# One row of value products, and a second layer that is entered without phases

## The reference, cut to what matters

```python
h = shift_token(x)                        # second half of the channels, one token down
q, k, v = split(h @ wqkv)                 # 8 heads of 64
q = l2norm(q) * qs;  k = l2norm(k) * ks
q, k = rotary_xpos(q, k)                  # x*cos*scale + rotate_half(x)*sin*scale
attn = softmax(mask(q @ k.T))             # 128 queries, own and preceding window of 128 keys
x = x + (attn @ v) @ wo
h = layernorm(shift_token(x)) @ w1 + b1   # 682 + 682 wide
x = x + (a * gelu(g)) @ w2 + b2
```

## Time and profile before

| | |
|---|---|
| runs | 1597.18, 1601.13, 1603.43 us; median 1601.13 |
| profiled execution | 1595.59 us, of which span 1593.7 us |
| busy share of the span | PE 93%, DVE 75%, ACT 65%, POOL 46% |
| chain that ended last | PE 79%, DVE 9%, ACT 4%, issue 4%, POOL 3% |
| mean granted TensorE clock | 0.971 of full speed |
| stage 0, attention 1, FFN 1 | to 269, to 707, to 918 us |
| attention 2, FFN 2 | 929 to 1370, to the end |

### The profile page before, as it was taken

How to read it: one execution, slowest core, us unless ns; L and a number is a source line. 1 busy time by engine, 2 the same in 40 slices (tenths; PEclk the granted TensorE clock), 3 DMA queues, 4 the chain that set the end, 5 groups by cost and what they waited for, 6 DMA issues and landing times.

```text
span 1593.7 us, 35524 instructions
## 1 busy us (share of the span) xinstructions
PE 1478.7 (93%) x10355; PEld 1209.0 (76%) x10355; DVE 1196.0 (75%) x3393; ACT 1030.2 (65%) x2610; POOL 735.2 (46%) x897
## 2 busy tenths in 40 slices
PE   7899991899999999979999949999999999799996
PEld 6468871688888888858888838888888888588885
DVE  6762786788888888885656458888888888766664
ACT  5223574688888888865454428888888888445553
POOL 4003255566555656532222145566665665244442
PEclk9999996999999999989999979999999999999998
DMA  5002134000000000002000020000000000000101
GB/s 176 1 1 85 77 113 116 16 7 5 5 5 5 5 5 5 5 8 88 8 13 7 14 63 5 6 5 5 5 5 5 6 5 6 30 27 28 53 27 53
DMA packets 57522, 44.04 MB, mean 28 GB/s; under 512 B 13214, under 2 KB 55386, under 8 KB 57442
## 3 DMA queue, kind: packets, MB, share of 16 engines
q1 hardware_dynamic: 57442, 43.07, 8.8%
HBM read 26.24 MB, written 8.39 MB: 22 GB/s over the span
## 4 chain that ended last, share of the span: by engine, by line
PE 79%; DVE 9%; ACT 4%; issue 4%; POOL 3%; DVEq 1%; ACTq 0%; DMA 0%; POOLq 0%; SPq 0%; PEldq 0%
PE bank L1892 8%; PE bank L1860 7%; PE bank L1806 7%; PE bank L1819 7%; PE bank L1725 6%; PE bank L1727 6%; PE bank L1726 6%; PE bank L1753 4%; PE bank L1955 4%; PE bank L1957 3%; PE bank L1956 3%; PE bank L1970 2%; PE bank L1605 2%; PE bank L1972 2%; PE bank L1971 2%
## 5 line engine op out<-in xcount | busy, mean ns | idle before, releaser
L1199 ACT ACTIVATE prob<-prob,neg_max 128x256 f32<-128x256 f32 x512 | 254.8, 502 | 0.2
L784 POOL TENSOR_TENSOR rnorm<-sumsq,neg_half 128x8 f32<-128x8 f32 x128 | 212.9, 1664 | 23.5 <-POOL sumsq L781 23.5
L798 POOL TENSOR_TENSOR qk_cos<-qk_cos,qk_sin 128x512 f32<-128x512 f32 x128 | 180.5, 1411 | 45.9 <-DVE qk_cos L2354 45.9
L1725 PE MATMUL bank<-wqkv_hi,hT_hi 128*128 128x512 f32 x384 | 177.3, 462 | 5.6 <-DVE hT_lo L2340 5.6
L1955 PE MATMUL bank<-h_hi,w_hi 128*128 128x512 f32 (+1 forms) x352 | 143.1, 406 | 12.5 <-POOL h_lo L839 12.5
L1727 PE MATMUL bank<-wqkv_hi,hT_lo 128*128 128x512 f32 x384 | 154.3, 402 | 0.0
L1726 PE MATMUL bank<-wqkv_lo,hT_hi 128*128 128x512 f32 x384 | 154.0, 401 | 0.0
L1121 ACT ACTIVATE qk_sq<-bank 128x512 f32<-128x512 f32 x128 | 76.9, 601 | 116.0 <-PE bank L1727 116.0
L1333 ACT ACTIVATE act_hi<-act_full 128x512 fp32r<-128x512 f32 x96 | 60.8, 634 | 137.3 <-DVE act_full L2677 137.3
L1232 ACT ACTIVATE pT<-bank 128x512 f32<-128x512 f32 x256 | 138.8, 594 | 10.6 <-PE bank L1892 3.4
L1892 PE MATMUL bank<-pT,v_sb 128*64 128x128 f32 x2048 | 140.2, 279 | 0.5 <-ACT pT L1232 0.5
(11 more groups left out here) (276 smaller groups left out, 3940.0 us busy)
## 6 DMA issues: line engine op xcount, KB each, us to landing
x_sb<-in_L_attn_hidden_states SPq DMA_DIRECT2D x8, 512.0 KB, 7.0
x_in<-in_L_attn_hidden_states SPq DMA_DIRECT2D x8, 512.0 KB, 4.8
x_scratch<-x_in SPq DMA_DIRECT2D x8, 512.0 KB, 3.0
f_x<-x_scratch SPq DMA_DIRECT2D x8, 512.0 KB, 4.0
out<-f_y SPq DMA_DIRECT2D x8, 512.0 KB, 3.0
raw<-in_L_ffn_w SPq DMA_DIRECT2D x6, 640.0 KB
hs<-x_sb SPq DMA_DIRECT2D x16, 224.0 KB
hs<-x_sb SPq DMA_DIRECT2D x64, 56.0 KB
```

Of the source, the lines that this page charges most:

```text
L784: pool.tensor_tensor(rnorm[:, part * HEADS:(part + 1) * HEADS], sumsq[:, which * HEADS:(which + 1) * HEADS], neg_half[:, 0:HEADS], ALU.pow ...
L1199: act.activation(prob[:, h], prob[:, h], ACT.Exp, bias=neg_max[:, h:h + 1], scale=-1.0, accum_out=psums[:, h:h + 1]).then_inc(exped, 1)
L1725: pe.matmul(bank[:, to], hT_hi[:, c], wqkv_hi[:, c, cols], start=(c == 0), stop=False)
```

## The change

It has three parts.

1. A second tile `pT_far` takes the place of spare memory, so that all four pieces of `probs_out` have a home, and PE does V1 V0 V2 V3 without a break.
2. The order of the pieces in `step` is new on every engine. PE projects block `n` in step `n` (before: `n-1`), weighs, turns and multiplies block `n-2` (before: `n-3`). POOL weighs two heads (before one), DVE three (before four). The orders of heads (HIDDEN, EXPED and so on) change with it.
3. Both barriers between layer 1 and 2 are gone. The tiles of the FFN lie elsewhere (`hn`, `h_full`, `gelu_sb`, `act_full`), so the tables can be made during the FFN: POOL makes the scales and all eight table pieces behind its last work of layer 1, then stages block 0. PE turns block 0 between the last two `down` of the last group, ACT and DVE take it out, and PE projects it right behind the last `down`. DVE's last `add_up` stands behind `lo(0)`. ACT clears the tiles in step 0. The last move into `hs` is waited for by POOL only before its loop.

```diff
@@ tiles
+        pT_far = place("pT_far", [P, 2, 4 * P])
-        place("spare", [P, 10 * P])
+        place("spare", [P, 2 * P])
@@ PE, step
-                    if live(n, 4):
-                        project_out(n - 4)
-                    if live(n, 1):
-                        project(n - 1, 1, qk_raw[1])
-                    if live(n, 2):
-                        scores(n - 2, 0)
-                    if live(n, 3):
-                        turn_probs(n - 3, 0)
-                        turn_probs(n - 3, 1)
-                    if live(n, 1):
-                        project(n - 1, 0, qk_raw[0])
-                    if live(n, 3):
-                        turn_probs(n - 3, 2)
-                        turn_probs(n - 3, 3)
-                        values(n - 3, 0)
-                        values(n - 3, 1)
-                    if live(n, 2):
-                        scores(n - 2, 1)
-                    if live(n, 3):
-                        values(n - 3, 2)
-                        values(n - 3, 3)
...
+                    if live(n, 1):
+                        turn_qk(n - 1, 0)
+                    if live(n, 0):
+                        transposes(n)
+                    if live(n, 3):
+                        project_out(n - 3)
+                    if live(n, 0):
+                        project(n, 1, qk_raw[1])
...
+                        values(n - 2, 1)
+                        values(n - 2, 0)
+                        values(n - 2, 2)
+                        values(n - 2, 3)
+                    if live(n, 1):
+                        scores(n - 1, 1)
+                    if live(n, 0):
+                        turn_qk(n, 1)
+                        project(n, 2, v_raw)
@@ PE, entry of layer 2
+                if lay:
+                    down(lay * NG - 1, FC - 2)
+                    pe.wait_ge(act_ready, FC * (lay * NG - 1) + FC - 1)
+                    transposes(0, ahead=True)
+                    down(lay * NG - 1, FC - 1)
+                    pe.wait_ge(act_ready, FC * lay * NG)
+                    pe.wait_ge(ffn_split, SPLITS * lay)
@@ POOL, end of FFN 1
-                    end_phase(pool, 4 + 2 * lay)
+                    scales(lay + 1)
+                    for a in range(2):
+                        for i in range(2):
+                            for h in range(2):
+                                table(a, i, h).then_inc(sc_made, 1)
+                    pool.wait_ge(hs_moved, moved_in(lay + 1) - 48)
+                    pool.wait_ge(w2_used, FC * (lay * NG + NG - 1))
@@ DVE, entry of layer 2
+                if lay:
+                    lo(0, ahead=True)
+                    add_up(lay * NG - 1, NG - 1)
+                    dve.wait_ge(sc_made, MADE + 2 * TABLES + 8)
@@ ACT, step (the part round the exponents)
+                    if live(n, 2):
+                        exponent(n - 2, 6)
+                    if live(n, 1):
+                        k_out(n - 1, 1 - i)
+                    if live(n, 2):
+                        exponent(n - 2, 7)
+                    if live(n, 0):
+                        hi(n)
```

More of the change, by code:

```diff
@@ L58 @@
 SPLITS = 4 + NG // 2
+TABLES = 6
 def hs_slot(t):
@@ new lines, in table @@
+                def table(a, i, h):
+                    operand = (raw[:, 2, 0:BPB * 64], sin_raw[:].rearrange("p a n -> p (a n)"))[a]
+                    return pool.tensor_tensor(rope[:, :, a, i, 32 * h:32 * h + 32], operand.rearrange("p (t k d) -> p t k d", t=BPB, k=2)[:, :, i, :],
+                                              sc_x[:, a, i, 32 * h:32 * h + 32][:, None, :].broadcast_to([P, BPB, 32]), ALU.mult)
+                if not lay:
+                    scales(0)
+                    for i, h in ((0, 0), (0, 1), (1, 0)):
+                        table(1, i, h)
+                    end_phase(pool, 3)
@@ L1278, in step @@
                         weigh(n - 2, 7)
+                        probs_out(n - 2, 0)
                         weigh(n - 2, 5)
-                for n in range(6):
-                    step(n, n % 2)
-                with act.Fori(3, NB // 2) as u:
+                        probs_out(n - 2, 1)
+                    if live(n, 1):
+                        exponent(n - 1, 1)
+                    if live(n, 0):
+                        square(n, 0)
+                    if live(n, 2):
+                        probs_out(n - 2, 2)
+                        probs_out(n - 2, 3)
+                    if live(n, 1):
+                        exponent(n - 1, 3)
+                        exponent(n - 1, 0)
+                        v_out(n - 1, 1 - i)
+                    if live(n, 2):
+                        values_out(n - 2)
+                    if live(n, 1):
+                        exponent(n - 1, 2)
+                for n in range(4):
+                    step(n, n % 2)
+                    if lay and n == 0:
+                        act.activation(warm[:], warm[:], ACT.Exp).then_inc(gate_exp, 1)
+                        act.wait_ge(w2_used, FC * NG * lay)
+                        clear()
+                with act.Fori(2, NB // 2) as u:
                     for i in range(2):
                         step(u * 2 + i, i)
-                for n in range(NB, NB + 3):
+                for n in range(NB, NB + 2):
                     step(n, n % 2)
@@ L1353, in _ @@
                     group(NG // 2 - 1, i, False, last)
-                if not last:
-                    act.activation(warm[:], warm[:], ACT.Exp).then_inc(gate_exp, 1)
-                    end_phase(act, 4 + 2 * lay)
-                else:
+                if last:
                     last_norm(NG - 1, 1, NG // 2)
@@ L1653, in _, with down, transposes @@
             end_phase(pe, 2)
+            def down(k, j):
+                w = fw(j)
+                pe.wait_ge(act_lo_ready, FC * k + j + 1)
+                if j == 0:
+                    pe.wait_ge(x_ffn, 1 + 2 * k)
+                for i in range(GB):
+                    to = bank[:, 4 + i // 2, (i % 2) * D:(i % 2 + 1) * D]
+                    tok = slice(i * P, (i + 1) * P)
+                    pe.matmul(to, act_hi[0:w, j % 3, tok], w2_hi[0:w, j], start=(j == 0 and i % 2 == 0), stop=False, skip_group_check=True)
+                    pe.matmul(to, act_hi[0:w, j % 3, tok], w2_lo[0:w, j], start=False, stop=False, skip_group_check=True)
+                    mm = pe.matmul(to, act_lo[0:w, j % 3, tok], w2_hi[0:w, j], start=False, stop=(j == FC - 1), skip_group_check=True)
+                mm.then_inc(w2_used, 1)
             for lay in range(DEPTH):
-                end_phase(pe, 3 + 2 * lay)
+                if not lay:
+                    end_phase(pe, 3)
                 k0 = lay * NB
-                def transposes(b):
+                def transposes(b, ahead=False):
+                    if lay and type(b) is int and b == 0 and not ahead:
+                        return
                     if follows(b, 2):
-                        pe.wait_ge(masked, nth(HIDDEN, k0 + b - 2, 7))
+                        pe.wait_ge(masked, nth(HIDDEN, k0 + b - 2, 4))
                     pe.wait_ge(h_staged, 2 * (k0 + b) + 2)
@@ L1930, in _ @@
                         step(u * 2 + i, i)
-                for n in range(NB, NB + 4):
+                for n in range(NB, NB + 3):
                     step(n, n % 2)
@@ L2707, in _ @@
                     group(NG // 2 - 1, i, False, last)
-                add_up(lay * NG + NG - 1, NG - 1)
-                if not last:
-                    end_phase(dve, 4 + 2 * lay)
-                else:
+                if last:
+                    add_up(lay * NG + NG - 1, NG - 1)
                     dve.wait_ge(x_ffn, 1 + 2 * NG * DEPTH)
```

353 lines of the change are left out of this document (173 added, 180 removed).

## The result

| | before | after |
|---|---|---|
| median of the runs | 1599.8 us | 1570.9 us (1569.2 to 1573.6) |
| ratio, with 95% interval | | 0.9822 [0.9806, 0.9837] |
| profiled execution | 1595.6 us | 1571.9 us |
| median in a second group of runs | 1598.3 us | 1570.6 us, ratio 0.9825 [0.9812, 0.9838] |

The forecast was 1577, the range 1568 to 1588. By profiled executions the forecast was 1571.8 and the profile has 1571.9. That they agree to 0.1 us is luck: the loop gave 3.8 us more than forecast, and the drain, the FFN stages and an untouched stretch took about as much away (see the table of stretches).

The account below looks back on a forecast made before the run. PE's own row of work was taken to bound both attention stages. Loop 8.4 + entry 12.9 + fill 1.5 + drain 1.0 = 23.8 us off the profiled 1595.6 gave 1571.8; with 5.5 for the median, 1577, range 1568 to 1588.

Parts of the forecast that it names:

- the loop: Attention loop in both layers: block falls from 13.00 to 12.85 us, 28 blocks per layer, 8.4 us saved.
- the drain: End of attention up to the FFN's first statistics: 0.5 us less per layer, 1.0 for both, bounds -2 and +3.
- the three tight places: Handoffs in the attention loop: T to PK, `probs_out` to V2 and V3, `v_out` to PV; spare 0.5 to 0.6 us.
- Rivals 1: Attention loop gets no shorter because a handoff takes over; only the other terms stay, 1586 us; chance 0.18.
- 2: Rival: attention loop slower, as the ring T, `hi`, `lo`, PK, S1, hides runs late; 1613 us at block 13.45; chance 0.06.
- 4: Rival: more gain, as the fill shortens by its upper bound and the drain too; 1570 us; chance 0.08.
- The row of values: Attention block on PE: one row of 32 value matmuls in place of two of 16 saves 0.15 us per block.
- 0.30, if a second border also goes away: Upper bound of the saving per attention block: two changes of array tiling removed, 0.15 us for each.
- The entry: Last `down` to layer 2's first projection: PK(0) at 918.3 and not 931.18, 12.9 us saved, bounds 11.1 and 13.3.
- The tables: On POOL during FFN 1: eight pieces at 1.71 us, done at 905.2; about 9 us spare after staging block 0.
- The fill: From PK(0) of layer 2: 1.2 us from a higher clock plus 0.3, in sum 1.5, bounds -1 and +4.
- I added 5.5 us: Step from profiled to median time: median of runs 1601.1 against profiled 1595.6, so 1571.8 became 1577.3.

Follow-up runs that it names:

- experiment 1: Changed kernel with the value products parted again (V1, V0, S1, V2, V3 on PE): 1602.8 us, ratio 1.0022 to the kernel before.
- experiment 3: Kernel before, old order and old entry, with `pT_far` added and V0 V1 V2 V3 in one row ahead of S1: 1677.3 us, ratio 1.0498.
- experiment 6: Changed kernel with the old entry into layer 2 (both barriers, tables behind the first, nothing turned ahead): 1583.7 us, ratio 0.9900 to the kernel before.
- (7): Changed kernel with block 0 of layer 2 turned behind the last `down`, not ahead of it: 1571.9 us, ratio 0.9841 to the kernel before.
- (8): Changed kernel, but POOL stages block 0, waits for the last `down`, then makes the tables: 1578.2 us, ratio 0.9882 to the kernel before.
- experiment 9: The changed kernel run once more, nothing altered, as comparison for later runs: 1570.6 us, ratio 0.9825 to the kernel before.
- experiment 11: Changed kernel with the first FFN group's statistics in DVE's wait for the last S1, roots on POOL before its last weighings: 1564.3 us, ratio 0.9785.
- experiment 12: Kernel of experiment 11 with one of the two `h_lo` moved to DVE: 1559.3 us, ratio 0.9750 to the kernel before.
- experiment 4: Changed kernel, PE's row the same, with its loop turning between T and WO as before: 1573.8 us, ratio 0.9839 to the kernel before.
- experiment 10: Changed kernel with `norm_full` of the first group ahead of the second `w1_rest` on DVE, both FFN stages: 1568.0 us, ratio 0.9811.

## Why the prediction was right, and where it was off

- **The bound.** PE's row sets the pace in both kernels, and the three tight places held: no idle time before T, PK, V2 or PV. Rivals 1 and 2 did not come, nor did 4: its surplus was to come from fill and drain. Experiments 1 and 3 show how near they were: with S1 gone from behind V3, or with the old order, handoffs cost 0.36 to 1.4 us per block.
- **The row of values.** 0.15 per block, forecast and measured. Read from starts and from the idle time of the weight loads, it was right by both.
- **The loop, 8.4 forecast, 12.2 measured: the term that was mis-sized.** The block fell by 0.24 and not by 0.15. By pieces: the values 0.15; the turn of the loop 0.055 in layer 1 and 0.04 in layer 2 (0.11 and 0.07 per turn, a turn every second block; it stood before WO, and now stands behind PV, where it costs nothing); 0.03 at the other borders, whose cause is open. The step that failed is thus that the prediction put the new order of PE's pieces, and with it the new place of the loop's turn, at nothing. The prediction's bound "0.30, if a second border also goes away" had room for it, but its cause was another. The row was there to be read: the earlier trace rows show WO 13.04 apart from 439.68 to 452.72 and 13.00 on average, and I averaged two kinds of block without asking why they differ.
- **The entry.** 12.9 forecast, 12.8 measured, and experiment 6 gives 12.8 back for it. The ahead-turned block is 1.6 of it (7). The tables' new place is worth some 7.6 (8), but that is the price of eight pieces on POOL alone, where the kernel before had three there and five on DVE, so what is left for the barriers (3.6, if the prices added) is not shown.
- **The tables.** 1.71 us each were forecast, 1.37 measured beside DVE and 1.23 without it. They end 13 us before PE wants block 0, and behind the staging 9 us of spare were left, as forecast. Two `act_lo` were slower by 1.1 and not three by 1.4, and it cost nothing.
- **The fill.** 1.5 forecast, 2.3 measured up to T(4) in layer 2 (3.5 in experiment 9), and -0.4 in layer 1 (0.7 in experiment 9). From PK(0) to the first WO of layer 2 it is 39.69 before, and 37.55 and 36.41 in two profiles of the changed kernel. In part that is how many projection matmuls start 0.43 us apart, at the lower level: 12 of 54 before, then 8 and 4. At 0.2 us each this is 0.8 us of either step; the rest is not traced. I could not forecast it better than its bounds.
- **The drain, 1.0 forecast, 0.0 measured.** I took what PE saved before the end for a gain. But from T of the last block on, the chain runs through DVE, ACT and POOL (PE's last turns of probabilities have 0.2 to 0.6 us of idle time before them, the last WO 0.7) and is as long as before. Experiments 11 and 12 show that the same stretch gives when that chain is shortened: 2.7 us in layer 1 and 3.4 in layer 2, then 3.9 and 4.7.
- **What was not forecast.** FFN 1 and FFN 2 got longer by 0.6 and 1.3 us, and the untouched stretch in front by 1.3. With the drain's missing 1.0 this takes back the loop's 3.8, so the sum of 23.8 came out right by chance.
- **The median.** I added 5.5 us, the distance of three runs' median from their profiled execution, to the forecast. In later groups the kernel before had medians of 1597.2 to 1599.5, and the changed kernel's lies 1 us under its profile. The distance is chance, not a scale; left out, the forecast was 1571.8 for a measured 1570.9. The medians differ by 28 to 29 us, though, and the profiled spans by 23.8. The runs show where those 4 to 5 us come from: the profiled execution of the kernel before is its fastest on record, 1595.6 us at a mean granted clock of 0.971, where its 50 timed runs in the four later groups lie at 1596.6 to 1603.3 with clocks of 0.966 to 0.970. The profile of the changed kernel, 1571.9 at 0.972, is on the slow side of its own runs (1568.1 to 1573.6, clocks up to 0.974). So the two profiles understate the gain. In which stretch the slower runs lose their time, no row shows.

## What to carry to other kernels

When one engine is busy all the time, cost its row piece by piece from start to start, and ask of every irregular piece why it differs: here about a fifth of the loop's gain was the place of the loop's turn. A piece that is moved also takes its cover along: S1 behind the values was worth 0.36 us per block as cover for `v_out`, more than the 0.15 that its own place cost. At the seams between stages look for the wait in front of the chain's engine: work that fits in it, like the statistics in DVE's 2.8 us, can be moved there, but look at what it then runs beside: in layer 1 of experiments 11 and 12 the last weighing then took longer, and 0.7 us of the gain went.

## What the runs showed of the hardware

- A turn of PE's loop costs 0.07 to 0.19 us when it falls between two short transposes and the output projection (0.11 and 0.07 in layers 1 and 2 of the kernel before, 0.19 in experiment 4), and nothing when it falls behind a projection of six 512-column matmuls. I have not tried other places. The Trainium skill (Advanced Engine Details and Errata, Control Flow Timing) gives about 108 ns for a compare and branch. Only the 0.11 of layer 1 before is near that; by the other rows the place of the turn decides.
- Elementwise operations on fp32 SBUF tiles slowed each other down on DVE and POOL in these pairs. Beside each other `act_lo` took 1.79 instead of 0.69, `w1_rest` 2.30 instead of 1.59, the two `h_lo` 3.84 instead of 3.06; a table piece took 1.37 instead of 1.23, and POOL's small `rstd` (128x4) 1.38 beside DVE's copy of `w_hi` instead of 0.23 (experiment 11). Moving work beside another engine's can so give back most of its gain, as in experiment 10.
- The stretch from PK(0) to the first WO of layer 2, with the same code, took 36.2 to 37.6 us in six profiles, with 4 to 11 of its projection matmuls at the lower clock level. In the two profiles of the changed kernel (first experiment 9 with 36.41 us, then the first profile with 37.55) the mean granted clock over 912 to 952 us is the same, 0.91. What differs is where the lower level falls: in experiment 9 more of it lies in 915 to 923 us, where PE is idle two thirds of the time, and in the slower profile more of it lies behind that, where PE has work:

```profile
915.00:923.00 8.00, 2.63 (x12) 1.93 (x11) 5.75 (x8) 4.24 (x7) 4.36 (x4) 0.79 0.26 34
923.00:952.00 29.00, 24.60 (x176) 19.74 (x174) 21.99 (x64) 19.25 (x54) 16.32 (x23) 0.94 0.27 78
```

```profile
915.00:923.00 8.00, 2.64 (x13) 1.84 (x12) 5.83 (x9) 4.24 (x7) 4.35 (x4) 0.96 0.25 34
923.00:952.00 29.00, 24.59 (x169) 19.61 (x168) 20.84 (x62) 17.80 (x49) 15.15 (x18) 0.89 0.26 78
```
